# Attention over eight images: the last unit's reciprocals spread by TensorE, the next image's load and statistics moved, value products in halves

## What is computed

```python
# layer 0
x = x + _L0_conv_ref(_gn(x), Wqkv, bqkv, Wout, bout)
# layer 1: windows of 8x8 pixels, 4 sampled points each, offsets by a small convolution,
# a bias from a small network (MLP), softmax over the 4 points, output projection
x = x + _L1_conv_ref(_gn(x), ...)

def _L0_conv_ref(x, Wqkv, bqkv, Wout, bout):
    xs = x.reshape(b, c, seq).transpose(0, 2, 1)          # seq = 1024
    q, k, v = jnp.split(xs @ Wqkv + bqkv, 3, axis=-1)     # 8 heads of 64
    scores = jnp.einsum('bhqd,bhkd->bhqk', q, k) / sqrt(64)
    attn = jax.nn.softmax(scores, axis=-1)
    out = jnp.einsum('bhqk,bhkd->bhqd', attn, v)
    out = out.transpose(0, 2, 1, 3).reshape(b, seq, c) @ Wout + bout
    return out.transpose(0, 2, 1).reshape(b, c, h, w)

def _gn(v, G=32, eps=1e-5):   # mean and variance of 16 channels x 1024 pixels
    ...
```

## Time and profile before

| | |
|---|---|
| median of 3 runs | 3468.84 us (3461.26 to 3483.75) |
| the profiled execution | 3447.59 us, of it the span of the profile 3445.5 us |
| TensorE busy (matmuls) | 3187.0 us, 92% |
| VectorE, ScalarE, GpSimd busy | 66%, 48%, 6% |
| mean granted TensorE clock | 0.974 of 2.4 GHz |
| chain that ended last | TensorE 75%, VectorE 10%, DMA 7%, ScalarE 4% |

### The profile page before, as it was taken

How to read it: one execution, slowest core, us unless ns; L and a number is a source line. 1 busy time by engine, 2 the same in 40 slices (tenths; PEclk the granted TensorE clock), 3 DMA queues, 4 the chain that set the end, 5 groups by cost and what they waited for, 6 DMA issues and landing times.

```text
span 3445.5 us, 51484 instructions
## 1 busy us (share of the span) xinstructions
PE 3187.0 (92%) x20640; PEld 2263.2 (66%) x20640; DVE 2278.8 (66%) x3031; ACT 1645.1 (48%) x2372; POOL 220.9 (6%) x165
## 2 busy tenths in 40 slices
PE   6998699899999999899998999989999999997978
PEld 5666576657766577666776667765776757765545
DVE  5665566576675676676666766668666586655765
ACT  3542455364552645445553545537454374553633
POOL 0000020000200010000200002000020000200200
...
DMA packets 137549, 214.30 MB, mean 62 GB/s; under 512 B 80929, under 2 KB 100900, under 8 KB 133444
## 3 DMA queue, kind: packets, MB, share of 16 engines
...
...
## 4 chain that ended last, share of the span: by engine, by line
PE 75%; DVE 10%; DMA 7%; ACT 4%; issue 3%; SPq 1%; POOL 0%; DVEq 0%; ACTq 0%
PE banks L666 12%; PE banks L681 12%; PE banks L650 11%; PE banks L611 9%; PE banks L621 8%; PE banks L840 4%; DMA recips_dram<-recips 4%; PE banks L850 3%; PE banks L841 3%; PE banks L842 3%; PE banks L711 2%; DMA wo_halves<-wo_split_dram 2%; DVE qk_halves L1546 2%; PE banks L916 2%; ACT exps L1075 2%
## 5 line engine op out<-in xcount | busy, mean ns | idle before, releaser
L1375 DVE TENSOR_REDUCE neg_max<-banks 128x1 f32<-128x1024 f32 x512 | 601.7, 1216 | 78.3 <-PE banks L650 77.2
L1075 ACT ACTIVATE exps<-banks,neg_max 128x1024 f32<-128x1024 f32 x512 | 564.8, 1111 | 152.5 <-DVE neg_max L1375 151.6
L1085 ACT ACTIVATE exps_turned<-banks 128x1024 f32<-128x1024 f32 x256 | 262.4, 1025 | 784.5 <-PE banks L666 784.5
L1384 DVE COPY exps_turned<-banks 128x1024 f32<-128x1024 f32 x256 | 313.2, 1223 | 453.8 <-PE banks L666 453.2
L666 PE MATMUL banks<-ident,exps 128*128 128x128 f32 x4096 | 554.5, 279 | 51.7 <-ACT exps_turned L1085 33.6
L666 PEld LDWEIGHTS banks<-ident,exps 128*128 128x128 f32 x4096 | 450.5, 142 | 207.3 <-issue 155.8
L650 PE MATMUL banks<-qk_halves 64*128 64x512 f32 x3072 | 432.4, 413 | 61.9 <-ACT exps L1075 56.3
L681 PE MATMUL banks<-exps_turned,values 128*64 128x256 f32 x4096 | 473.5, 384 | 13.7 <-issue 9.5
L681 PEld LDWEIGHTS banks<-exps_turned,values 128*64 128x64 f32 x4096 | 287.9, 137 | 163.0 <-issue 36.4
L650 PEld LDWEIGHTS banks<-qk_halves 64*128 64x128 f32 x3072 | 283.2, 187 | 147.7 <-issue 109.3
L1546 DVE SCALAR_TENSOR_TENSOR qk_halves<-banks,qk_halves 128x1024 fp32r<-128x1024 f32 x256 | 301.8, 1218 | 70.4 <-ACT qk_halves L1122 70.2
...
## 6 DMA issues: line engine op xcount, KB each, us to landing
...
recips_b<-recips_dram SPq DMA_DIRECT2D x256, 64.0 KB, 3.6
exps_turned<-in_x SPq DMA_DIRECT2D x32, 512.0 KB, 10.3
...
x_image<-in_x SPq DMA_DIRECT2D x7, 2048.0 KB, 10.3
```

The source lines that it names most:

```text
L1075: freed(act.activation(PB[:, 2 * h + n % 2], slot(("s", m, i)), ACT.Exp, bias=NM[:, m:m + 1], accum_out=SS[:, m:m + 1]), ("s", m, i))
L1375: dve.tensor_reduce(NM[:, m:m + 1], slot(("s", m, i)), AX.X, ALU.max, negate=True).then_inc(mx, 1)
L1384: dve.tensor_copy(PT[:, n // 2 % 2, 1, :, P * j:P * j + P], TB.rearrange("p s (k q) -> p (s k) q", k=4)).then_inc(t_free[1], 1)
```

## The change

Six things are done:

- The reciprocals of the last unit (u = 15) no longer go through DRAM. `spread_recips` on TensorE multiplies each column of RC, broadcast to 64 columns, with the identity, which puts the 128 values along the free axis of MB on 64 partitions; `keep_recips` on ScalarE copies them to `RB[:, 1]`. SyncE's loop runs over 15 units, and `recips(15)` on VectorE comes a little sooner.
- The load of the next image (u = 10) is issued ahead of the way back of unit 10's reciprocals.
- The statistics of the next image are dealt anew over VectorE's steps 25 to 27: all four tiles are done by step 25, with `group_channels`; `group_variance` is behind the copy of step 26, `normalise(0)` and `(1)` ahead of the copy of step 27. `key_blocks` is behind the copy of step 26, `x_low(1)` behind that of step 29. ScalarE's `x_high` comes one step sooner.
- The group sums go to MB instead of OB, and `similarities(0)` waits until they are read.
- From step 24 on a value product is done in halves, the first in the even step, the second in the odd one behind it; so is unit 14's, whose second half is in step 31, between `turn(31, 0)` and `values(0)`.
- `outputs(15)` on VectorE stands ahead of `add_value_bias(0)`.

```diff
--- before.py
+++ after.py
@@ -214,7 +214,7 @@
         TB_ALL = TB.rearrange("p s n -> p (s n)")
         OB = PS[:, 6]
         MB = PS[:, 7]
-        GSO = OB[:, 256:264]
+        GSO = MB[:, 256:264]
         GSM = MB[:, 0:8]
         OM_ALL = PS[:, 6:8].rearrange("p s n -> p (s n)")
 
...
@@ -463,11 +465,14 @@
             sp.dma_start(WOR[:], wo0.rearrange("(t p) n -> p t n", p=P)).then_inc(wo_raw, 16)
 
             def recips_around(u, i):
-                b, k = u % 2, u // 2
+                b, k, uses = u % 2, u // 2, i * (OUTS // 2 - u % 2)
                 sp.wait_ge(rc_done, i * OUTS + u + 1)
                 sp.dma_start(rc_dram[b].rearrange("m q -> q m"), RC[:, b], allow_slow_non_contiguous=True)\
                     .then_inc(rc_out[b], 16)
-                sp.wait_ge(rc_out[b], i * 128 + 16 * k + 16)
+                if u == 10 and i + 1 < B:
+                    wait_full(sp, ("s", 47, i))
+                    sp.dma_start(X[:], x[i + 1].rearrange("(t p) n -> p t n", p=P)).then_inc(x_in, 16)
+                sp.wait_ge(rc_out[b], 16 * (uses + k + 1))
                 wait_after(sp, ot_done, i * OUTS + u - 1)
                 for h in range(2):
                     sp.dma_start(RB[D * h:D * h + D, b],
@@ -509,7 +514,7 @@
                     sp.dma_start(yj[:, t], XR[:, t]).then_inc(y_out, 16)
 
             for i in range(B):
-                for u in range(OUTS):
+                for u in range(OUTS - 1):
                     recips_around(u, i)
                     if u == 5 and i:
                         rows_to_dram(i - 1)
@@ -523,9 +528,6 @@
                     if i + 1 < B:
                         if u in (9, 11):
                             load_wq(u // 2 - 4, i + 1)
-                        if u == 10:
-                            wait_full(sp, ("s", 47, i))
-                            sp.dma_start(X[:], x[i + 1].rearrange("(t p) n -> p t n", p=P)).then_inc(x_in, 16)
                         if u == 12 and i:
                             sp.wait_ge(kvt_full, 2 * i)
                             sp.dma_start(WV[:].bitcast(F32), wv_dram).then_inc(wv_in, 16)
@@ -683,6 +685,17 @@
                 if half == 1:
                     mm.then_inc(av_full, 1)
 
+            def spread_recips(i):
+                pe.wait_ge(rc_done, i * OUTS + OUTS)
+                wait_after(pe, vz_done, i)
+                for j in range(2):
+                    for h in range(2):
+                        m = 2 * h + j
+                        mm = pe.matmul(MB[D * h:D * h + D, P * j:P * j + P],
+                                       RC[:, 1, m:m + 1].broadcast_to([P, D]), IDENT[:], start=(j == 0), stop=True,
+                                       skip_group_check=True)
+                mm.then_inc(rbc_full, 1)
+
             def piece(n, i):
                 p, which = piece_of(n)
                 w, c = which // 2, 512 * (which % 2)
@@ -759,6 +772,8 @@
 
             def similarities(f, j):
                 pe.wait_ge(kz_done, j + 1)
+                if f == 0 and j + 2 < B:
+                    pe.wait_ge(gn_var, 2 * j + 4)
                 wait_after(pe, sim_done, 2 * j + f)
                 for r in range(4):
                     for t in range(CT):
@@ -960,8 +975,9 @@
                     if n == 0:
                         piece(0, i)
                     if n >= 2 and n % 2 == 0:
-                        for half in range(2):
-                            value_product(n // 2 - 1, half, i)
+                        value_product(n // 2 - 1, 0, i)
+                    if (2 <= n < 24 and n % 2 == 0) or (n > 24 and n % 2):
+                        value_product(n // 2 - 1, 1, i)
                     if piece_of(n + 1):
                         piece(n + 1, i)
                     if i + 1 < B and n == STEPS - 1:
@@ -993,6 +1009,7 @@
                         similarities(1, i - 1)
                     if i and n == 30:
                         sampled_values(i - 1)
+                spread_recips(i)
                 for half in range(2):
                     value_product(OUTS - 1, half, i)
                 if i + 1 < B:
@@ -1179,6 +1196,11 @@
                     act.wait_ge(wo_out, 16 * k)
                 act.activation(WOS[:, 0], WOR[:], ACT.Copy).then_inc(wo_hi, 1)
 
+            def keep_recips(i):
+                act.wait_ge(rbc_full, i + 1)
+                act.wait_ge(ot_done, i * OUTS + OUTS - 2)
+                act.activation(RB[:, 1], MB[:, 0:256], ACT.Copy).then_inc(rb_copied, 1)
+
             def attended_high(t, i):
                 act.wait_ge(ot_done, i * OUTS + 4 * (t + 1))
                 if t == 0 and i + 1 < B:
@@ -1216,9 +1238,9 @@
                     if n + 1 < STEPS:
                         for h in range(2):
                             exp(n + 1, h, i)
-                    if i + 1 < B and n in (28, 29):
-                        x_high(2 * (n - 28), i + 1)
-                        x_high(2 * (n - 28) + 1, i + 1)
+                    if i + 1 < B and n in (27, 28):
+                        x_high(2 * (n - 27), i + 1)
+                        x_high(2 * (n - 27) + 1, i + 1)
                     if n == 0:
                         high_piece(0, i)
                     if piece_of(n + 1):
@@ -1231,8 +1253,10 @@
                         log(i - 1)
                     if not i and n in (4, 10):
                         wo_high(n // 10)
-                for t in range(CT):
+                for t in range(CT - 1):
                     attended_high(t, i)
+                keep_recips(i)
+                attended_high(CT - 1, i)
                 act.wait_ge(gn2_ready, i + 1)
                 if not i:
                     act.wait_ge(wo_out, 32)
@@ -1387,12 +1411,15 @@
             def recips(u, i):
                 for h in range(2):
                     wait_emptied(dve, ("s", 4 * u + 2 + h, i))
-                wait_after(dve, rc_out[u % 2], i * 128 + 16 * (u // 2))
+                wait_after(dve, rc_out[u % 2], 16 * (i * (OUTS // 2 - u % 2) + u // 2))
                 dve.reciprocal(RC[:, u % 2].rearrange("p (h j) -> p h j", h=2),
                                SS[:, 4 * u:4 * u + 4].rearrange("p (j h) -> p h j", h=2)).then_inc(rc_done, 1)
 
             def outputs(u, i):
-                dve.wait_ge(rb_in[u % 2], i * 256 + 32 * (u // 2) + 32)
+                if u == OUTS - 1:
+                    dve.wait_ge(rb_copied, i + 1)
+                else:
+                    dve.wait_ge(rb_in[u % 2], 32 * (i * (OUTS // 2 - u % 2) + u // 2 + 1))
                 dve.wait_ge(av_full, i * OUTS + u + 1)
                 if u == 8 and i:
                     dve.wait_ge(rows_out, 16 * PTS * i)
@@ -1676,12 +1703,12 @@
                         sampled(0, i - 1)
                     if i and n == 26:
                         sampled(1, i - 1)
-                    if i and n == 27:
-                        key_blocks(i - 1)
                     if i and n == 28:
                         sim_rows(0, i - 1)
                     if i and n == 29:
                         sim_rows(1, i - 1)
+                    if n == STEPS - 1:
+                        recips(OUTS - 1, i)
                     if i and n == 31:
                         value_blocks(i - 1)
                     if i + 1 < B:
@@ -1691,28 +1718,31 @@
                             group_parts(X, 1)
                         if n == 25:
                             group_parts(X, 2)
-                        if n == 26:
                             group_channels(group_parts(X, 3))
                         if n == 27:
-                            group_variance(2 * i + 2, GSO)
+                            dve.wait_ge(gn_rstd, 2 * i + 2)
+                            normalise(0)
+                            normalise(1)
                         if n == 28:
                             normalise(2)
                             normalise(3)
                         if n == 29:
                             x_low(0, i + 1)
-                            x_low(1, i + 1)
                         if n == 30:
                             x_low(2, i + 1)
                             x_low(3, i + 1)
                     if n % 2:
-                        recips(n // 2, i)
+                        if n < STEPS - 1:
+                            recips(n // 2, i)
                         if n >= 3:
                             outputs(n // 2 - 1, i)
                     copy_turned(n, i)
-                    if i + 1 < B and n == 27:
-                        dve.wait_ge(gn_rstd, 2 * i + 2)
-                        normalise(0)
-                        normalise(1)
+                    if i + 1 < B and n == 26:
+                        group_variance(2 * i + 2, GSO)
+                    if i and n == 26:
+                        key_blocks(i - 1)
+                    if i + 1 < B and n == 29:
+                        x_low(1, i + 1)
                     if n == 0:
                         low_piece(0, i)
                     if piece_of(n + 1):
```

(2 more changed lines are left out.)

2 lines of the change are left out of this document (added).

## The result

The changed kernel took 3460.47 us (median of 20 runs, 3454.7 to 3469.34) beside 3474.35 us of the kernel before (20 runs, 3458.71 to 3484.14): a ratio of 0.9963, 95% interval 0.9953 to 0.9973. That is no change by the bound of 1%, and 39 us above the forecast of 3421, outside its range. Two more comparisons, each with its own runs of the kernel before, gave 0.9957 [0.9933, 0.9981] and 1.0001 [0.9990, 1.0011].

The account below looks back on a forecast made before the run. TensorE was taken as three quarters of the chain, so gains come only from its idle time or slow clock. Terms of 21.4 + 11.9 + 13 + 1.2 + 4.5 + 6.5 - 3.5 - 7 = 48 us gave 3421 us, range 3388 to 3448.

Parts of the forecast that it names:

- WO0's wait: First output projection, images 0 to 6: TensorE's wait for the output weights goes whole, 21.4 us gained.
- the projection's slow start: Output projection behind that wait, six images: low clock at its start goes too, 11.9 us gained.
- The last image: Scores of step 24 to the projection in the last image: 71.2 us shrink to 58.1, 13 us gained.
- Image 3: Unit 14's late arrival and slow product in image 3 go, since the last unit's reciprocals leave the queue: 4.5 us gained.
- Steps 24 to 31: Images 1 to 6: halved products fill TensorE's gaps, but VectorE takes most back; 0.2 us an image, 1.2 us gained.
- image 0: Steps 24 to 31 without sampling work: last product at 56.9 instead of 63.3 us, 6.5 us gained.
- the slow clock: Low clock behind the new waits at steps 26 and 31: half an occurrence an image, 7 us lost.
- The load ahead of the way back: Next image's load ahead of unit 10's returning reciprocals: 0.5 us an image, 3.5 us lost; bounds nothing and 17.
- Rival 3: Way back behind a slow load makes unit 10's multiply 12.2 us late in seven images: 3503 us; chance 0.03.
- Rival 2: Load wholly ahead of unit 10's reciprocals, 13.5 us more than taken: 3434 us, 3442 with slow clock; chance 0.12.
- Rival 1: VectorE becomes the bound in steps 24 to 31, 14 to 34 us of gain stay: 3435 to 3455; chance 0.17.
- rival 5: Halves fill the gaps better, 3.5 us an image more and no clock price: 3390 us; chance 0.14.

Follow-up runs that it names:

- tail alone: Kernel before with only the last unit's reciprocals spread by TensorE, kept by ScalarE, last multiply ahead of the value bias; ratios 0.9866, 0.9834, 0.9859, 0.9876.
- load behind: Changed kernel with the next image's load issued behind unit 10's way back again; ratios to the kernel before 0.9893 and 0.9898.
- last group: One-chip runs beside the kernel before: changed kernel 1.0001, it with the image load behind unit 10's way back 0.9898, only the last unit's reciprocals changed 0.9876.
- the run with two queues: Changed kernel with the next image's load issued by GpSimd on a DMA queue of its own; 3430.84 us, ratio to the kernel before 0.9953.

## Why the prediction was wrong

**Term by term**, forecast and measured:

- **WO0's wait, 21.4 us, and the projection's slow start, 11.9 us:** both went whole, in the seven images. WO0 left at 1053.31 in image 2, 17 us ahead of the projection, as forecast. The tail alone, these terms and most of the next, gave 46.4, 55.1, 50.1 and 42.8 us in four comparisons, where 40 were expected.
- **The last image, 13 us:** 8.9 in the profiled execution of the result, 12.4 and 12.5 in two others. In the first, unit 14's reciprocals took 13.3 us from issue to use (3116.62 to 3129.90) where the prediction had 12.5, and left later than worked out; the product began at 57.0, not 53.5, and took 5.36 us, at the low clock. In the others it began at 54.5 and 54.6, took 3.67, and the projection waited 0.61 and 0.36 us for WO0: the term was right, path and size. With the tail alone, whole products, four profiled executions took 60.9 to 64.0 us from the same scores to the projection, and four with the halves and the load behind or unmoved 59.5 to 60.3, so the halves bring a microsecond or more here.
- **Image 3, 4.5 us:** its late unit 14 of before was an event of that execution. In the changed kernel image 3 took 67.4 us, where it had 67.2, with 2.75 us of the load's wait in it; so some of the 4.5 may be there, under that.
- **Steps 24 to 31, 1.2 us, image 0, 6.5, and the slow clock, -7:** the two new waits stand where they were put: 2.40 us at the turn of step 26 (forecast 2.4) and 1.81 at step 31 (forecast 2.1), the half product behind the second 3.52 us in place of 1.95. Two smaller ones were not forecast, 0.72 us at the turn of step 28 and 1.11 at step 30. With the load behind, images 4 and 6 of the last group took 65.8 and 65.9 us to the last product, where 63.85 were forecast; before, image 2 took 64.0. Image 0's gain did not come: 63.7 and 63.9 us with the load behind, where 56.9 were forecast from 63.3. Together the three terms are +0.7 in the forecast; halves and statistics cost 8.3 and 12.1 us in the runs.
- **The load ahead of the way back, -3.5 us:** measured -35.0, -42.5 and -49.2 us on three kernels. **This is the step that failed.** The prediction took it from bounds of 0 and 17 and stayed near nought, for the reason that the way back "already lay beside the load nearly whole and TensorE did not wait". That read the row the wrong way round. Before, the way back was issued 1.1 us ahead of the load and so had hardly anything in front of it: in image 2 it was used at 980.05, while the engines moved 78 GB/s from 977 to 979 and 401 from 979 to 984, when the load went. To lie beside a load that comes later costs little; to come later than the load costs 8.5 to 13.1 us in place of 3.1 to 5.5 from issue to use (with the load behind, last group). The pair in the other order was not in the trace, as the prediction itself said.

The upper bound of 17 was too low as well. It had the way back end 3.6 us after a load of 10.3 us. The load took 14.9 on the median and 18.7 in image 2, with the way back 1.4 us behind it: it was issued while unit 10's own way out was still being written, 512 single numbers of four bytes, and it landed late behind its data. And the bound counted the wait alone, where the runs show that half as much again (16.8 us beside 31.5) goes to the low clock behind it. The prediction's other limit held: it let the multiply start up to 0.1 us ahead of the scores of step 24, it came 8.5 behind them, and TensorE waited 8.55.

**The rivals.** Rival 3 had the mechanism, the load whole and the way back behind it, in every image. It had priced each way back at 12.2 us of TensorE's time; the rows show 2.75 to 8.57, 41.9 us in all and the low clock with it. It expected 3503; the change's own gains and the smaller wait put it at the level of the kernel before. Its first multiply, forecast for 993.4 with the scores of step 24 at 981.30, came at 993.88 with them at 985.37, so 8.5 us behind them where 12.1 were expected. Rival 2 was the same case at 13.5 us, with the rule of the Trainium skill (DMA: Bandwidth & Descriptors, section Queues, rings and completion order) that a queue's descriptors are consumed in ring order. The rows with both in one queue agree with it: the way back is there 12.5 us after its issue and 1.4 behind the load's landing in image 2, though its first half came before that landing. The rule is not the whole cause, as the run with two queues shows. Rival 1 (VectorE as the bound) named a wait that is there: of the 88.3 us, 53.1 stay with the load put back, where 17.0 were before. With its load behind the way back, the change gives 3407.94 beside 3442.43 us, 34.5 us or 1.0%. Without the load's term the forecast's sum is 51.5, so it was some 17 us too high apart from the failed step.

The range failed with the same step: it reached from rival 5 to most of rival 1, and rivals 2 and 3, one mechanism at three prices, were given 0.15 together.
